# Moving the value projections of both attention layers into the start of the attention phase, with the loads, the last unit and the narrow exponentials rearranged

## What is computed

```python
# layer 0: 32 heads of 16, causal, rotary, plus an adapter of 10 prefix tokens
q, k, v = split(x @ w_attn.T)                    # each 1024 x 512
y = softmax(causal(rope(q) @ rope(k).T / 4)) @ v
y = y + gating * softmax(rope(q) @ ak.T / sqrt(512)) @ av
x = layernorm(x + y @ w_proj.T)
# a lookup layer (left out here), then layer 1: 32 query heads, 8 key/value heads of 16
q, k, v = x @ Wq, x @ Wk, x @ Wv                 # 512, 128, 128 wide
x = layernorm(x + softmax(causal(rope(q) @ rope(k).T / 4)) @ repeat(v, 4) @ Wo)
# a SwiGLU layer (left out here)
```

## Time and profile before

| what | value |
|---|---|
| median of three runs | 1014.57 us (1011.73 to 1017.09) |
| the profiled execution's own time | 1011.6 us |
| its span in the profile | 1009.9 us |
| PE busy | 915.9 us (91%) |
| DVE busy | 669.6 us (66%) |
| ACT busy | 503.5 us (50%) |
| POOL busy | 278.4 us (28%) |
| mean granted TensorE clock | 0.938 of full speed |

### The profile page before, as it was taken

One profiled execution on the slowest core, in us unless ns is written; L12 is line 12 of the kernel. 1 busy time (PEld: TensorE's weight loads), 2 busy tenths in 40 slices (PEclk: granted clock), 3 DMA queues, 4 the chain that ended last, 5 costly groups with the idle time before them and its releaser, 6 DMA issues. The chain is left out here.

```text
span 1009.9 us, 15158 instructions
## 1 busy us (share of the span) xinstructions
PE 915.9 (91%) x5334; PEld 503.2 (50%) x5334; DVE 669.6 (66%) x1177; ACT 503.5 (50%) x1134; POOL 278.4 (28%) x527
## 2 busy tenths in 40 slices
PE   6887989999999998988698599999999889799997
PEld 4555853433444432855365233434444338577766
DVE  5975547877788760965748577877778518455464
ACT  5221322776766665224612146777767652367630
POOL 2454141223223321033345122223223212013200
PEclk9997985999999999988789779999999999899999
DMA  9332060221212110200023400111100010321001
GB/s 323 94 95 79 1 149 25 55 53 54 65 49 63 47 40 7 99 1 1 0 75 112 111 22 25 37 40 39 41 26 2 2 42 1 136 82 64 22 32 53
DMA packets 50029, 57.14 MB, mean 57 GB/s; under 512 B 8928, under 2 KB 39712, under 8 KB 49952
## 3 DMA queue, kind: packets, MB, share of 16 engines
q1 hardware_dynamic: 48320, 55.75, 18.4%
q10 hardware_dynamic: 1632, 0.39, 0.2%
HBM read 43.41 MB, written 12.32 MB: 55 GB/s over the span
## 5 line engine op out<-in xcount | busy, mean ns | idle before, releaser
L1001 DVE TENSOR_REDUCE mx<-psum 128x1 f32<-128x512 f32 (+3 forms) x640 | 370.6, 631 | 114.5 <-PE psum L866 70.1
L861 PE MATMUL psum<-arena_s 96*128 96x512 bf16 (+3 forms) x768 | 226.5, 349 | 9.6 <-DVE mx L1001 5.5
L947 ACT ACTIVATE arena_p<-psum 128x512 f32<-128x512 f32 (+1 forms) x384 | 185.1, 591 | 92.7 <-PE psum L886 61.6
L886 PE MATMUL psum<-arena_s 99*128 99x512 bf16 (+3 forms) x768 | 204.4, 335 | 8.5 <-ACT arena_p L947 3.3
L947 ACT ACTIVATE arena_x<-psum 128x128 f32<-128x128 f32 (+2 forms) x384 | 133.9, 439 | 88.6 <-PE psum L886 65.7
L861 PEld LDWEIGHTS psum<-arena_s 96*128 96x128 bf16 x768 | 71.2, 99 | 124.4 <-DVE mx L1001 70.9
L886 PEld LDWEIGHTS psum<-arena_s 99*128 99x128 bf16 x768 | 66.9, 98 | 100.9 <-ACT arena_p L947 34.4
L1052 POOL TENSOR_SCALAR_AFFINE_SELECT arena_p<-arena_p 128x256 f32<-128x256 f32 x128 | 50.9, 408 | 204.2 <-ACT arena_p L947 204.2
L259 PE MATMUL psum<-x_h,w 128*128 128x512 f32 x224 | 87.9, 456 | 10.8 <-DVE w L476 7.6
L866 PE MATMUL psum<-maskb,ident_b 128*128 128x128 bf16 (+1 forms) x384 | 96.5, 251 | 0.0
L904 PE MATMUL psum<-arena_p,v_grp 128*32 128x512 f32 (+1 forms) x768 | 91.5, 597 | 0.0
(11 more groups left out here) (202 smaller groups left out, 1203.6 us busy)
## 6 DMA issues: line engine op xcount, KB each, us to landing
q_parts<-arena_p SPq DMA_DIRECT2D x48, 128.0 KB
arena_s<-q_parts SPq DMA_DIRECT2D x32, 192.0 KB, 2.9
arena_s<-k_parts SPq DMA_DIRECT2D x96, 64.0 KB, 2.3
ff_raw<-in_w_in SPq DMA_DIRECT2D x11, 512.0 KB, 3.6
arena_s<-q_parts SPq DMA_DIRECT2D x32, 128.0 KB, 3.0
k_parts<-arena_p SPq DMA_DIRECT2D x30, 128.0 KB
arena_w<-in_w SPq DMA_DIRECT2D x12, 256.0 KB, 6.5
ff_wd_raw<-in_w_down SPq DMA_DIRECT2D x1, 2560.0 KB, 11.3
```

Source lines behind the costliest of these rows:

```text
L861: last = pe.matmul(psum[:, bank, width * n:width * n + width], q_st[0:KS, b % NS, 512 * r + P * i:512 * r + P * i + P], k_st[0:KS, g % NK, ...
L886: pe.matmul(psum[:, 2 * (n % 2) + t, o:512], k_st[0:KM, g % NK, at:at + P], q_st[0:KM, u % NS, 512 * r + o:512 * r + 512], start=True, sto ...
L947: act.activation(pr[n % NP_RING][:, t, o:512], psum[:, 2 * (n % 2) + t, o:512], ACT.Exp, scale=scale).then_inc(exp_ready, 1)
L1001: dve.tensor_reduce(mx[:, b % 2, kc, col:col + 4 * len(heads) - 3:4], src, AX, ALU.max)\
```

## The change

Seven edits are made together.

1. The value projections leave the projection phase (layer 1) and the adapter (layer 0). They are now issued by PE in the attention phase, spread evenly over the first 42 of the 48 entries of the ramp (`v_product`): 96 matmuls of 512 columns in layer 0 and 24 in layer 1, where two groups of four transposes (`v_turn`) follow behind entries 44 and 47. ACT copies the results; the first scores wait for these copies.
2. The adapter's order holds only scores, T, y and the second exponential, which now stands behind T of tile 2. `load_first` no longer waits.
3. In the attention phase SyncE waits for the last value product before the loads that overwrite the value weights.
4. `load_max(u)` is issued by ACT as soon as its T entry is due by `issued_by(u, 2 * b - 6)`, ahead of the exponential of step b.
5. POOL's `split_max` is placed by `issued_by(u, 2 * b - 4)` without the floor at zero, so one step later; `load_v(0)` and the third memset of the "-1" rows come behind the second split, and the memsets are fp32 of half the elements.
6. The last group's units are swapped: the long unit, then the short one (`UNITS`).
7. Exponentials of steps of width 256 and 128 are one ACTIVATE over two heads.

```diff
+UNITS = [(c, g) for g in range(NG - 1) for c in range(CH)] + [(1, NG - 1), (0, NG - 1)]
...
-    order = [("scores", 0), ("V", 0), ("V", 1), ("scores", 1)]
+    order = [("scores", 0), ("scores", 1)]
     for n in range(NT):
         order.append(("T", n))
-        if n < 3:
-            order += [("V", 2 * n + 2), ("V", 2 * n + 3), ("y", n)]
-        elif n > 3:
+        if n == 2:
+            order.append(("exp", 1))
+        if n:
             order.append(("y", n - 1))
...
-            sp.wait_ge(turn_ready, turns.index(("V", NT - 1)) + 1)
             stacked.load_first(sp)
...
     def issued_by(u, slot):
 
-        done = sum(unit_columns[0:u]) + unit_columns[u] * slot // (4 * n_tiles[steps[u][0]])
+        if slot < 0 and u > 0:
+            return issued_by(u - 1, slot + 4 * n_tiles[steps[u - 1][0]])
+        done = sum(unit_columns[0:u]) + unit_columns[u] * max(0, slot) // (4 * n_tiles[steps[u][0]])
...
+            ramp = issued_by(0, 0)
+            n_products = 3 * KC * V_DONE
+            for e in range(ramp):
+                b = next(x for x in range(NU + 1) if issued < first_entry[x + 1])
+                entry(issued, b, lists[b][issued - first_entry[b]])
+                issued += 1
+                done = min(n_products, n_products * e // (ramp - 6))
+                for i in range(done, min(n_products, n_products * (e + 1) // (ramp - 6))):
+                    v_product(i)
+                if layer == 1 and e in (ramp - 4, ramp - 1):
+                    v_turn(0 if e == ramp - 4 else 1)
...
+                if o >= 256:
+                    act.wait_ge(scores_ready, 2 * n + 2)
+                    act.activation(pr[n % NP_RING][:, :, o:512], psum[:, 2 * (n % 2):2 * (n % 2) + 2, o:512],
+                                   ACT.Exp, scale=scale).then_inc(exp_ready, 2)
+                    return
...
             for u in range(NU):
                 for b in range(2 * n_tiles[steps[u][0]]):
+                    while sent < NU and turn_entry(sent) < issued_by(u, 2 * b - 6):
+                        load_max(sent)
+                        sent += 1
                     exp(u, b)
                     if u and b == 3:
                         copy_o(u - 1)
-                    if u + 1 < NU and b == 4:
-                        load_max(u + 1)
...
+            def minus(slot):
+                pool.memset(k_st[KS:KM, slot, :].bitcast(F32), two_minus).then_inc(rows, 1)
+                pool.wait_ge(rows, slot + 1)
...
                     while split < NU and min(first_entry[split + 1] + 3, first_entry[NU]) \
-                            <= issued_by(u, max(0, 2 * b - 4)):
+                            <= issued_by(u, 2 * b - 4):
                         split_max(split)
                         split += 1
+                        if split == 2:
+                            pool.wait_ge(v_copied, V_COPIED)
+                            load_v(0)
+                            pool.wait_ge(vg_ready, 1)
+                            minus(2)
```

More of the change, by code:

```diff
@@ L303, in cut_of @@
         kind, k, n0 = piece
+        if kind == "w" and n0 == 2 * C:
+            return [w[:, k, n0:n0 + 512], *[a[:, k, :] for a in m["wv_hl"]]]
         return [a[:, k, n0:n0 + 512] for a in ((x_raw, xh, xl) if kind == "x" else (w, wh, wl))]
@@ L595, in _ @@
             for what, n in order:
+                if what == "exp":
+                    continue
                 if what == "scores":
@@ L749, in attention @@
     n_tiles = [4 * (c + 1) for c in range(CH)]
-    steps = [(c, g) for g in range(NG) for c in range(CH)]
+    steps = UNITS
     NU = len(steps)
@@ L821, in _ @@
                 stacked.load_k(sp, 1, c)
-            stacked.load_q(sp, 3)
+            if layer == 0:
+                stacked.load_q(sp, 3)
+            sp.wait_ge(v_ready, V_DONE)
+            if layer == 1:
+                stacked.load_q(sp, 3)
             stacked.load_q(sp, 4)
@@ L854, in entry @@
                 i, heads, kc, width = what
-                g, c = divmod(b, CH)
+                c, g = steps[b]
                 if number == first_entry[b]:
                     pe.wait_ge(q_loaded[b % NS], 48 * (b // NS + 1))
-                    pe.wait_ge(k_loaded[g % NK][c], stacked.k_count * (g // NK + 1))
+                    for half in range(c + 1):
+                        pe.wait_ge(k_loaded[g % NK][half], stacked.k_count * (g // NK + 1))
                 for n, r in enumerate(heads):
@@ L879, in scores @@
                     if u == 0:
-                        pe.wait_ge(rows, NK)
+                        pe.wait_ge(v_copied, V_COPIED)
+                    if u < 2 * NK and u % 2 == 0:
+                        pe.wait_ge(rows, u // 2 + 1)
                 for t in range(2):
@@ L917, in maxima, with v_product, v_turn @@
                     issued += 1
-            maxima(0, 0)
+            def v_product(i):
+                tile, step = divmod(i, 3 * KC)
+                k, n = divmod(step, 3)
+                a, b = ((0, 0), (0, 1), (1, 0))[n]
+                xs, ws = v_from["x"], v_from["w"]
+                if layer == 0:
+                    bank, lhs, rhs = tile % 4, xs[a][:, k, P * tile:P * tile + P], ws[b][:, k, :]
+                    if step == 0 and tile >= 4:
+                        pe.wait_ge(v_copied, tile - 3)
+                else:
+                    bank, lhs, rhs = tile, ws[a][:, k, C + P:C + 2 * P], xs[b][:, k, 512 * tile:512 * tile + 512]
+                last = pe.matmul(psum[:, bank, :], lhs, rhs, start=step == 0, stop=step == 3 * KC - 1)
+                if step == 3 * KC - 1:
+                    last.then_inc(v_ready, 1)
+            def v_turn(c):
+                pe.wait_ge(v_copied, c + 1)
+                for t in range(4):
+                    last = pe.transpose(psum[:, 2 + c, P * t:P * t + P],
+                                        v_from["v_T"][:, c, P * t:P * t + P], v_from["ident"][:, :])
+                last.then_inc(v_ready, 1)
+            ramp = issued_by(0, 0)
[9 more added lines that the diff above has]
+                    v_turn(0 if e == ramp - 4 else 1)
             for u, kt in blocks[0:2]:
@@ L959, in load_max @@
                     .then_inc(max_loaded[u % NS], 16)
-            load_max(0)
+            for t in range(V_DONE):
+                act.wait_ge(v_ready, t + 1)
+                if layer == 0:
+                    act.copy(v_tok[:, t, :], psum[:, t % 4, :]).then_inc(v_copied, 1)
+                else:
+                    act.copy(v_from["v_T"][:, t, :], psum[:, t, :]).then_inc(v_copied, 1)
+                if t == V_DONE // 2:
+                    load_max(0)
+            sent = 1
+            for c in range(CH if layer == 1 else 0):
+                act.wait_ge(v_ready, CH + c + 1)
+                act.copy(v_tok[:, 4 * c:4 * c + 4, 0:P],
+                         psum[:, 2 + c, :].rearrange("p (t f) -> p t f", f=P)).then_inc(v_copied, 1)
             for u in range(NU):
                 for b in range(2 * n_tiles[steps[u][0]]):
+                    while sent < NU and turn_entry(sent) < issued_by(u, 2 * b - 6):
+                        load_max(sent)
+                        sent += 1
                     exp(u, b)
@@ L979, in _ @@
             for b in range(NU + 1):
-                if b == NU:
+                if b == NU and steps[b - 1][0] == 1:
                     join_max(b - 1)
@@ L1030, in split_max @@
                 pool.tensor_tensor(low, md[:, :], mid, ALU.subtract).then_inc(max_ready, 1)
-            for s in range(NK):
-                pool.memset(k_st[KS:KM, s, :], -1.0).then_inc(rows, 1)
-            pool.wait_ge(rows, NK)
-            load_v(0)
+            two_minus = float(np.uint32(0xBF80BF80).view(np.float32))
+            def minus(slot):
+                pool.memset(k_st[KS:KM, slot, :].bitcast(F32), two_minus).then_inc(rows, 1)
+                pool.wait_ge(rows, slot + 1)
+            minus(0)
+            minus(1)
             split = 0
```

90 lines of the change are left out of this document (33 added, 57 removed).

## The result

| | median | runs | ratio to before |
|---|---|---|---|
| before | 1014.21 us | 1011.73 to 1017.09 | |
| after | 1060.94 us | 1052.54, 1059.93, 1061.95, 1072.38 | 1.0432 [1.0362, 1.0502] |

The change makes the kernel 4.3% slower. Executions that were disturbed are left out of every ratio: that of 1072.38 us here (without it the median is 1059.93 us), and one of 1154.77 us in experiment 7. The forecast was 1048.3 us. The profiled execution is the one of 1052.54 us, span 1050.8 us, so between the two profiled executions lie 40.9 us, between the medians 46.7.

The account below looks back on a forecast made before the run. PE was taken to bound steady attention, DVE the ramps; the adapter was not PE-bound. Terms -11.8 + 3.0 + 8.1 + 0.8 - 2.4 + 2.0 + 2.0 + 24 + 12 - 1 = +36.7 gave 1048.3 us, range 1012 to 1066.

Parts of the forecast that it names:

- The DMA in short units: Five short units per layer: ACT's DMA holds up step 3, so PE waits 2.4 us each, +24 us.
- wait is hidden: Rival: DMA in short units issued before PE asks for step 3, so no stall cost; 1012.3 us, chance 0.09.
- faster than before: Rival: wait hidden and value products fit into the ramps without clock loss; 1002.2 us, chance 0.12.
- The clock behind these stalls: Steady attention: half clock on PE after the short-unit stalls, 1.2 us each, +12 us, between 0 and 34.
- The rival with no loss of clock: Short-unit stalls occur but PE's clock stays up; 1036.3 us, chance 0.25.
- the rival with a cold stretch of 6.8 us behind every wait: Each short-unit stall is followed by a full 6.8 us at half clock; 1070.3 us, chance 0.12.
- Adapter: Adapter before attention 0: value tiles removed, -11.8 us at the same clock, +3.0 for colder clock.
- Ramp of attention 0: Layer 0 ramp: value products make PE the bound, 34.8 us against 26.7, +8.1 us, between 5 and 12.
- Start of unit 0: Unit 0, layer 0: DMA ahead of the first exponential +0.8 us, full clock from denser PE work -2.4 us.
- Start of layer 1: Behind the last ramp entry of attention 1: second v_turn, copy, DMA and table load, together +2.0 us.
- ramp of attention 1: Layer 1 ramp: DVE stays the bound, part of PE's cold clock shows, +2.0 us, between 0 and 6.
- The rest: Pairs, swapped last units and a DMA wait in the last long unit, together -1 us, between -3 and +3.

Follow-up runs that it names:

- experiment 7: e1 plus a one-column exponential at ACT's start of attention 1, loading the exponential's table early; 1023.7 us, ratio 1.0065.
- e1: The changed kernel with the DMA of the next maxima in short units issued behind step 4 again, as before; 1021.94 us, ratio 1.0061.
- e2: The kernel before with only the new rule for the DMAs of the maxima added; 1070.2 us, ratio 1.0564.
- e3: The changed kernel with the DMA in short units one step later, ahead of step 4 in place of step 3; 1035.93 us, ratio 1.0212.
- e4: The changed kernel with all exponentials single again, no pairs; 1064.1 us, ratio 1.0506.
- e5: e1 with the value products of both layers back in the adapter and projection 1; 1018.85 us, ratio 1.0042.
- e6: e1 with the value products of layer 0 alone back in the adapter; 1019.76 us, ratio 1.0063.
- e10: e9 with the value products of both layers back, leaving only pairs, POOL's order and memsets of the change; 1014.49 us, ratio 1.0004.
- e8: e1 with the old order of units, the last two not swapped; 1020.51 us, ratio 1.0061.
- e9: e8 with the old DMA rule, behind step 4, in every unit including unit 0; 1016.28 us, ratio 1.0038.

## Why the prediction was right in direction, and where its sizes were off

**The DMA in short units (+24): right.** Per wait 2.4 us was forecast and 2.41 measured, from T to the products 4.57 us against 4.6 (2.16 + 2.4). ACT's idle stretch of "3.5 us or more" is 3.76, put down to DVE (the profile names a reduction; DVE's copy ends at 204.60 and the DMA starts at 204.63). e1, e2 and e3 show that the position of the DMA is the cause, by removal, addition and dose. The rivals "wait is hidden" and "faster than before" fall with the same rows: the scores of step 5, the second row of 256 columns, start at 206.04, 2.4 us behind T and not under 1.

**The clock behind these stalls (+12): right in kind, too small for the median.** In the profiled execution of after two of the five waits of each layer are followed by 3.4 us at half clock, worth 1.6 us each: 4 x 1.6 = 6.4 us, under the 12. But that is the fastest of four executions, and the median is 8.4 us above it at a mean clock of 0.922 to 0.927 where it has 0.934. The pair of medians says 39.0 - 24.1 = 15 us, an estimate that takes in whatever else differs between those executions. The rival with no loss of clock, 1036.3 us, is thereby out. The median lies about halfway between the forecast and the rival with a cold stretch of 6.8 us behind every wait, 1070.3 us. Its mechanism isn't in the profiled execution (3.4 us, behind two waits in five); the other executions have no profile, and how their cold stretches lie is open.

**Adapter (-8.8 with its clock): 1.6 us short.** The first matmul of attention 0 came 7.2 us earlier, not 9 to 12. PE in before, at the second half of the scores, and in after:

```profile
105.60 3.69 PE L602 MATMUL psum<-arena_f,arena_o 128*128 128x80 f32 x32
```

```profile
103.22 7.12 PE L586 MATMUL psum<-arena_f,arena_o 128*128 128x80 f32 x32 [3.11 <-DVE arena_o L637]
...
120.45 0.83 PE L605 MATMUL psum<-ident,arena_o 128*80 128x128 f32 x3 [4.11 <-DVE arena_o L644]
```

The second half of the scores runs in a stretch at 0.51 and takes 7.12 us in place of 3.69, and so the second softmax ends at 120.3 us in place of the 118.3 of the sum. PE idles 3.11 and 4.11 us in this phase and is at half clock for 17 us of it. The step that failed is "it could therefore end at 118.3": with the value tiles gone, the softmax waits for scores that no longer run at full clock. By the medians of the eight and the five profiled executions the move gives 7.4 us here; e4, the worst, is at half clock for 20.5 us from 97.8 on and for 17.1 from 125.1 on, and starts attention 0 at 137.57.

**Ramp of attention 0 (+8.1): 1.5 us short.** 36.34 us in place of 34.8, the same to 0.01 us in every profiled execution with the products but e4, whose ramp starts cold (38.44). PE has 35.94 us of work in it, where the sum had 33.7: the term was mis-sized in what a product beside an entry costs PE, and is inside its own bounds. The ramp that it was set against could itself have been some 1.6 us shorter, as e5, e6 and e10 show.

**Start of unit 0 (+0.8 - 2.4): wrong in sign.** It became +0.9 us. Its two terms behave differently, as e8 and e9 show. The start at full clock is worth 2.65 us in e9, as forecast; that the products give it is not shown, since e10 has 13.50 us without them (and e5 and e6, which have the DMA in front, 16.3 and 16.1). The DMA ahead of the exponential, taken at 0.86 us from the spacing of two rows, costs 2.9: the 1.2 us that the exponentials start later, and the half clock behind PE's wait. A step was costed by its own length and not by what the wait does to the clock, which the next paragraph of the forecast did for the other units.

**Start of layer 1 (+2.0): 2.6 us short.** In after (ACT, then PE):

```profile
613.97 0.59 ACT L999 COPY v_tok<-psum 128x512 f32<-128x512 f32 x1 [0.91 <-PE psum L927]
614.14 0.73 ACTq L985 DMA_DIRECT2D arena_s<-mT  x1
614.90 1.28 ACT L974 ACT_TABLE_LOAD   x1 [0.35 <-issue]
616.20 1.09 ACT L974 ACTIVATE arena_p<-psum 128x512 f32<-128x512 f32 x2
```

```profile
616.85 0.34 PE L874 MATMUL psum<-arena_s 99*128 99x384 bf16 x1 [1.18 <-ACT arena_p L974]
```

```profile
618.30:625.10 6.80, 6.78 (x31) 2.33 (x31) 2.40 (x4) 2.96 (x7) 2.44 (x6) 0.51 0.05 14
```

Copy, DMA and table load stand in line ahead of the first exponential, as forecast; it starts 3.09 us behind T where it started 0.88 behind (593.82 against 592.94, with the load long done): +2.2. The missing 2.4 us are again half clock behind PE's wait, 6.8 us at 0.51. The ramp of attention 1 itself cost 0.4 us and not 2.0 (0.5 to 1.2 in the eight other profiled executions with the products in it): it ran at 0.92 and DVE stayed the bound, busy 24.40 of 25.88 us.

**The rest (-1): wrong in sign.** The end of the attentions takes +2.2 and +0.9 us, and e8 puts 2 us of it on the swapped units of layer 0. The forecast had named the DMA ahead of the last long unit at "some 1.4 us" and set the saved join against it. It should have stood as a loss. Pairs and memsets at nothing: the times of e4 and e10 agree.

**The sum.** That the forecast of +36.7 us lies within 4.2 us of the 40.9 between the profiled executions is in part luck. By the rows of the ledger 12.4 us of terms that came out too small stand against 8.2 that came out too large, the larger part of these the clock of the steady stretches.

**The move of the value products as a whole** was worth about nothing, as the sum had it (-8.8 + 8.1 - 2.4 in layer 0). In e9 layer 0 comes out at -7.5 + 9.6 - 2.7 = -0.6 us and layer 1 at some +4, 4.5 of it at the start of unit 0. By its interval e9 is 0.1 to 0.65% slower than before and e10 is level with it. Between the two profiled executions e10 reaches T of unit 2 in layer 0 at 177.10 us and e9 at 180.41, so with POOL's new order in both the move looks like a loss of 3 us there. How much of those 2 to 3 us is the move and how much is chance in the clock stays open, since the intervals of e9 and e10 overlap.

## What to carry to other kernels

The DMA that ACT issues was part of ACT's ordered stream here: while it waited for data, the exponential behind it waited 3.76 us. Before moving one earlier, look at when its data comes and at who needs the next instruction in that stream; here a transfer that nobody was short of was issued 2.4 us too soon in ten places. And a wait put on TensorE in a dense stretch should be priced with the clock that may follow it, which here added some 15 us to 24 by the medians, and 6 in the profiled execution.

## What the runs showed of the hardware beyond that

Half clock followed waits of PE that were short and broken. In after the piece at 0.52 from 239.4 us on came behind these two waits, with matmuls between them:

```profile
237.65 0.66 PE L874 MATMUL psum<-arena_s 99*128 99x256 bf16 x2 [1.55 <-ACT arena_p L974]
239.01 0.28 PE L874 MATMUL psum<-arena_s 99*128 99x128 bf16 x2 [0.48 <-ACT arena_x L969]
```

The same two waits in unit 2 (1.58 and 0.47 us) were followed by none, so the same work gets either clock. Executions of one kernel differ with it: the three of after that the ratio uses have 0.934, 0.927 and 0.922 at 1052.54, 1059.93 and 1061.95 us. Such a spread needs no new wait, though: the 29 executions of before beside e9 go from 0.933 at 1011.26 us to 0.921 at 1019.84.

The cold stretches also go with where the products stand. The ramp of attention 0 with them ran at 1.00 in seven of eight profiled executions, and the twelve executions of e9 have a mean clock of 0.929 to 0.943, against 0.921 to 0.935 for the 29 of before beside them, at a longer time: a higher mean clock was no sign of a faster kernel.

POOL's memset of the rows of -1 went from 10.41 us for three of 3x4096 bf16 to 1.83 us each for 3x2048 fp32 (3.66 for two), the same bytes in half the elements. POOL in before, PE in before, and POOL in after:

```profile
138.16 10.41 POOL L1033 MEMSET arena_s<- 3x4096 bf16 x3 [33.99 <-POOLq L244]
```

```profile
150.38 0.27 PE L850 MATMUL psum<-ident_b,mst 128*48 128x128 bf16 x1 [2.03 <-POOL mst L1030]
```

```profile
130.91 3.66 POOL L1077 MEMSET arena_s<- 3x2048 f32 x2 [26.93 <-POOLq L246]
```

It went by the number of elements (about 0.85 and 0.89 ns each), not by bytes. Before, it was on the path, which the forecast overlooked where it gave the memsets slack: POOL's split of the first maxima stood behind them and a copy, and PE waited 2.03 us for it ahead of the first T entry. With the new memsets and POOL's new order this wait is gone, and where the products aren't in the ramp (e5, e6, e10) the ramp takes 24.9 to 25.3 us against 26.7 before and in e2. With the products in it PE is the bound and nothing of this shows, and the median of e10 doesn't tell it from chance.
